# Where a mean aggregation's two projections are computed, and who casts its adjacency, in a four-block graph network

## What is computed

```python
x = x + gnn0(layernorm(x), adj)        # attention over the graph
x = x + ffn0(layernorm(x))             # 64 experts' routing with capacity 256, one shared feed-forward
x = x + gnn1(layernorm(x), adj)
x = x + ffn1(layernorm(x))             # 8 experts, top 2

def ffn0(h):    # idx, p: two best of softmax(h @ router_w.T); keep: place in its expert < 256
    y = gelu(h @ w1.T + b1) @ w2.T + b2                      # 256 -> 1024 -> 256
    return y * sum_over_two(where(keep, p, 0))

def gnn1(h, adj):
    deg = adj.sum(axis=1, keepdims=True) + 1e-5
    return relu((adj / deg) @ h @ W_neigh.T + b_neigh + h @ W_self.T + b_self)

def ffn1(h):    # w = softmax over the two best logits of h @ Wg + bg
    a, g = split(h @ W1[e] + b1[e]); return sum_e w_e * ((silu(a) * g) @ W2[e] + b2[e])
```

## Time and profile before

| | us |
|---|---|
| three runs | 1263.65, 1255.98, 1261.61 |
| median | 1261.61 |
| profiled execution, its own time | 1258.48 |
| its span | 1256.6 |
| attention | to 405 |
| feed-forward, ahead of its chunk loop | 405 to 431 |
| feed-forward, chunks and the end behind them | 431 to 596.4 |
| self projection | 596.4 to 640.9 |
| aggregation, to its last product | 640.9 to 840.4 |
| aggregation, behind its last product | 840.4 to 886.8 |
| experts and combination | 886.8 to 1256.6 |

### The profile page before, as it was taken

The page is one execution under the profiler, slowest core; times in us unless marked ns, Lnnn a source line. Parts: engine busy times, 40 slices in busy tenths (PEclk is TensorE's granted clock), DMA queues, the critical chain, the costliest instruction groups (busy, mean ns, idle before and its releaser), DMA issues. The chain is left out here.

```text
span 1256.6 us, 24125 instructions
## 1 busy us (share of the span) xinstructions
PE 1058.0 (84%) x7768; PEld 857.3 (68%) x7769; DVE 848.2 (67%) x1916; ACT 691.8 (55%) x752; POOL 121.2 (10%) x122
## 2 busy tenths in 40 slices
PE   4759999999999799898789999981199999999930
PEld 3548888888888688787568888871056666666620
DVE  7469999999994656766734676675255565565526
ACT  2669999999982777774455555530033333333310
POOL 1000000000000000000000132224011211211210
PEclk9889999999999699999889999995599999999975
DMA  9937777777700212110357678721621111111127
GB/s 286 286 113 229 218 246 216 234 224 220 242 18 1 77 68 101 68 35 1 126 210 290 263 285 309 296 89 64 261 111 54 50 54 54 50 54 54 47 85 261
DMA packets 71546, 186.91 MB, mean 149 GB/s; under 512 B 7777, under 2 KB 57824, under 8 KB 62144
## 3 DMA queue, kind: packets, MB, share of 16 engines
q1 hardware_dynamic: 51152, 138.38, 33.5%
q10 hardware_dynamic: 11616, 29.76, 6.5%
q0 software_dynamic: 8720, 17.99, 4.9%
HBM read 140.75 MB, written 45.35 MB: 148 GB/s over the span
## 5 line engine op out<-in xcount | busy, mean ns | idle before, releaser
L586 PE MATMUL PS<-G,PT 128*128 128x256 f16 x2028 | 230.3, 273 | 0.0
L586 PEld LDWEIGHTS PS<-G,PT 128*128 128x128 f16 x2028 | 198.8, 98 | 22.8
L1343 PE MATMUL sum<-H,adjTh 128*128 128x257 f16 x676 | 154.4, 276 | 7.7 <-ACT adjTh L1290 7.7
L1345 PE MATMUL sum<-H,adjTh 128*128 128x256 f16 x676 | 154.4, 275 | 0.0
L1748 DVE SCALAR_TENSOR_TENSOR hb<-ePsH,w_unscale,eb 128x1024 f32<-128x1024 f32 x59 | 75.7, 1284 | 86.4 <-PE ePsH L1669 86.4
L1669 PE MATMUL ePsH<-W,xT_hi 128*128 x472 | 122.5, 382 | 4.7 <-DVE xT_lo L1739 4.7
L1705 ACT ACTIVATE xT_hi<-ePsX 128x256 f16<-128x256 f32 x59 | 22.6, 384 | 177.6 <-PE ePsX L1658 177.6
L1689 PE MATMUL ePsY<-W,actT 128*128 x472 | 111.6, 380 | 0.2 <-issue 0.2
L573 PE MATMUL PS<-ident,probs 128*128 128x128 f32 x676 | 90.0, 280 | 22.2 <-DVE PT L434 20.5
L434 DVE SCALAR_TENSOR_TENSOR PT<-PS,PT 128x1024 f16<-128x1024 f32 x104 | 103.4, 1016 | 4.4 <-ACT PT L283 4.4
L573 PEld LDWEIGHTS PS<-ident,probs 128*128 128x128 f32 x676 | 76.3, 144 | 31.9 <-issue 23.9
(11 more groups left out here) (271 smaller groups left out, 1931.2 us busy)
## 6 DMA issues: line engine op xcount, KB each, us to landing
adjf<-adj_dram SPq DMA_DIRECT2D x26, 1664.0 KB, 8.2
adjTf<-adjT_dram SPq DMA_DIRECT2D x26, 1664.0 KB, 8.7
slot_rows<-blank SPq DMA_DIRECT2D x26, 1028.0 KB, 11.2
c_w<-eW_dram ACTq DMA_DIRECT2D x8, 1024.0 KB, 5.0
xs<-slot_rows SPq DMA_DIRECT2D x59, 128.5 KB, 2.0
d_stage<-eW_dram ACTq DMA_DIRECT2D x7, 1024.0 KB, 8.0
results<-results_dram ACTq DMA_DIRECT2D x12, 512.0 KB, 9.4
eb<-eb_dram SPq DMA_DIRECT2D x1, 4096.0 KB, 13.9
```

What stands on the lines that cost most here:

```text
L586: mm = nc.tensor.matmul(acc[u][:, 0:D], left, right, start=(j == 0 and n == 0), stop=(j == T - 1 and n == 2))
L1343: nc.tensor.matmul(acc[u][:, 0:D + 1], left, H[:, j, 0:D + 1], start=(j == 0), stop=False, skip_group_check=True)
L1345: mm = nc.tensor.matmul(acc[u][:, 0:D], left, H[:, j, D + 2:2 * D + 2], start=False, stop=(j == T - 1), skip_group_check=True)
```

## The change

What it does, in five parts:

1. The program `normalised_projection` is gone. `capacity_ffn` loads W_self and W_neigh (side by side in `wsn`, 512 columns) and their biases, takes their norm in the same sum as the others, and splits them. For each pair of tiles r = 0 to 12: `residual(r)` with the moments, `row_deviation` (a square root on ScalarE), `normalise_rows`, `turn_rows` (four transpositions into psT), `rows_hi` (ScalarE) and `rows_lo` (VectorE), `project_rows` (for each tile six products 512 columns wide into psR[s], s = 0 or 1, one buffer for each tile of the pair), `neighbour_hi` (ScalarE) and `own_and_lo` (VectorE), which write the projected neighbour rows into H and the self projection with biases into `own`. `row_group(c)` is the two pairs 2(c-8), 2(c-8)+1: in chunk c their residual and normalisation, in chunk c+1 the rest.
2. Aggregation multiplies the adjacency with the projected rows: `residual(i)` is sum times 1/degree plus `own`, then relu and addition to X. `turn_mean` and `project` go.
3. The adjacency is loaded by GpSimd's transfers from the f32 array straight into f16 buffers, four of them (`NADJ`), and the cast on ScalarE goes. GpSimd issues them from aggregation's own start, two loads ahead of each pair's scatters.
4. Behind the products the pairs follow at less distance; rows are normalised once into one of four buffers (`NROW`), the second copy is ScalarE's (`second_copy`); the counts have a PSUM tile of their own.
5. The experts' scales (`expert_ffn` changes in the index of `w_unscale` alone): one for all eight experts, from the columns' largest magnitudes (`expert_peak` on VectorE, chunks 2 to 9) in place of the eight squares; the second weights' squares are new (`second_square`, ScalarE, chunks 10 and 11 and behind the loop). The first activation buffer G of the feed-forward is single in place of double, and its weights and row halves lie in the room of W1, which is allocated earlier; `own` and H serve as scratch.

The feed-forward's loops after it, cut:

```diff
+            def project_rows(r):
+                pe.wait_ge(rowT_lo, r + 1)
+                for s in range(2):
+                    wait(pe, own_ready, 2 * (r - 1) + s + 1)
+                    for n, (left, right) in enumerate(((0, 0), (0, 1), (1, 0))):
+                        for k in range(KD):
+                            mm = nc.tensor.matmul(psR[s][:, :], rowT[r % 2][left][:, k, s * P:(s + 1) * P],
+                                                  wsn_p[right][:, k, :], start=(n == 0 and k == 0),
+                                                  stop=(n == 2 and k == KD - 1))
+                    mm.then_inc(proj_done, 1)
...
-            for c in range(NCH + 1):
+            for c in range(NCH + 3):
                 for b in range(4):
                     if c < NCH:
                         if b == 0:
                             pe.wait_ge(lo_ready, c + 1)
                         hidden_part(c, b)
...
+                    for r in row_group(c - 1)[b % 2:b % 2 + 1]:
+                        if b < 2:
+                            turn_rows(r)
+                        else:
...
+                            project_rows(r)
...
-                    if c > 0:
+                    if 0 < c <= NCH:
...
                         output_part(c - 1, b)
```

ScalarE in chunk c:

```diff
                 gelu(c, 0)
                 gelu(c, 1)
                 gelu_hi(c, 0)
...
-                if 2 <= c < 2 + E1:
-                    expert_square(c - 2)
...
+                if c == 10:
+                    second_square(0)
+                if c == 11:
+                    second_square(1)
...
+                for r in row_group(c - 1)[0:1]:
+                    rows_hi(r)
+                for r in row_group(c - 2)[1:2]:
+                    neighbour_hi(r)
                 gelu(c, 2)
                 gelu_hi(c, 1)
                 gelu(c, 3)
                 gelu_hi(c, 2)
+                for r in row_group(c - 1)[1:2]:
+                    rows_hi(r)
                 gelu_hi(c, 3)
+                for r in row_group(c - 1)[0:1]:
+                    neighbour_hi(r)
+                row_deviation(c)
```

VectorE in chunk c:

```diff
                 gelu_lo(c, 1)
...
-                if c >= 8:
-                    residual(4 * c - 32, 4 * c - 30)
+                if 2 <= c < 2 + E1:
+                    expert_peak(c - 2)
+                for r in row_group(c - 2)[1:2]:
+                    own_and_lo(r)
+                for r in row_group(c - 1)[0:1]:
+                    rows_lo(r)
+                for r in row_group(c)[0:1]:
+                    residual(r)
                 gelu_lo(c, 2)
...
-                if c >= 8:
-                    residual(4 * c - 30, 4 * c - 28)
+                for r in row_group(c - 1)[1:2]:
+                    rows_lo(r)
+                for r in row_group(c)[1:2]:
+                    residual(r)
                 gelu_lo(c, 3)
+                for r in row_group(c - 1)[0:1]:
+                    own_and_lo(r)
...
+                invert_deviation(c)
+                for r in row_group(c):
+                    normalise_rows(r)
```

Aggregation:

```diff
-                dve.wait_ge(proj_ready, t + 1)
-                v.tensor_tensor(own[:, t, :], psF[u][:, 0:D], own[:, t, :], ALU.add).then_inc(out_ready, 1)
+                dve.wait_ge(rdeg_ready, i + 1)
+                v.scalar_tensor_tensor(own[:, i, :], acc[u][:, 0:D], rdegree[u][:, :], own[:, i, :], ALU.mult,
+                                       ALU.add).then_inc(out_ready, 1)
...
+            def load(i):
+                if live(i):
+                    wait(pool, acc_ready, i - NADJ + 1)
+                    pool.dma_start(adjh[i % NADJ][:, :], adjv[i, :, :]).then_inc(adj_in[i % NADJ], 16)
...
+            for i in range(NADJ - 1):
+                load(i)
+            for i in range(0, TOTAL, 2):
+                load(i + NADJ - 1)
+                load(i + NADJ)
+                if live(i - 6):
+                    scatter(i - 6)
```

More of the change, by code:

```diff
@@ new lines, in normalise_rows, with rows_lo @@
+            def normalise_rows(r):
+                dve.wait_ge(row_ready, r // 2 + 1)
+                wait(dve, rows_turned, r - 1)
+                for s in range(2):
+                    i = 2 * r + s
+                    v.tensor_scalar(h[:, r % 2, s, :], X[:, i, :], moments[:, i, 0:1], row_rstd[:, i:i + 1], ALU.subtract,
+                                    ALU.mult).then_inc(rows_done, 1)
+            def rows_lo(r):
+                dve.wait_ge(rowT_hi, r + 1)
+                v.scalar_tensor_tensor(rowT[r % 2][1][:, :, :], psT[r % 2][:, :].rearrange("p (k n) -> p k n", k=KD), H_SCALE,
+                                       rowT[r % 2][0][:, :, :], ALU.mult, ALU.subtract).then_inc(rowT_lo, 1)
@@ L1264, in mean_aggregation @@
+        slots_ready, token_ready, copy_ready = sem("d_slots"), sem("d_token"), sem("d_copy")
+        scattered = [sem(f"d_scattered{q}") for q in range(NROW)]
+        stage_in, split_hi, split_done = sem("d_stage_in"), sem("d_split_hi"), sem("d_split")
         block = ctx.enter_context(nc.Block())
@@ L1332, in _, with deviation, second_copy @@
-            act.wait_ge(ones_set, 1)
-            for i in range(0, TOTAL, 2):
-                body(i)
+            def deviation(i):
+                act.wait_ge(moments_ready, i + 2)
+                wait(act, rstd_ready, i // 2)
+                nc.scalar.activation(std[:, :], moments[(i // 2) % 2][:, :, 1], ACT.Sqrt, bias=eps[:, :]).then_inc(std_ready, 1)
+            def second_copy(i):
+                act.wait_ge(h_ready, i + 2)
+                for u in range(2):
+                    nc.scalar.copy(rows[:, row_slot(i), u, 1, 0:D], rows[:, row_slot(i), u, 0, 0:D]).then_inc(copy_ready, 1)
@@ L1336, in _, with products @@
         @block.tensor
         def _(pe):
-            def products(t, u):
-                pe.wait_ge(half_ready, t + 1)
-                wait(pe, agg_ready, t - 1)
-                for j in range(T):
-                    left = adjh[u][:, j * P:(j + 1) * P]
+            def products(i, first, last):
+                u = i % 2
+                if first == 0:
+                    pe.wait_ge(adj_in[i % NADJ], 16 * (i // NADJ) + 16)
+                    wait(pe, out_ready, i - 1)
+                for j in range(first, last):
+                    left = adjh[i % NADJ][:, j * P:(j + 1) * P]
@@ L1453, in row_norm @@
[L1453 to L1459 removed]
+                    dve.wait_ge(stats_done, i + u + 1)
@@ L1503, in write_slots @@
[L1503 to L1507 removed]
+                m = i // 2
```

757 lines of the change are left out of this document (391 added, 366 removed).

## The result

The changed kernel took 1316.53 us, the median of four runs (1315.12 to 1318.29), the kernel before 1259.94 (1255.98 to 1263.65): a ratio of 1.045, 95% interval 1.041 to 1.049. It is 4.5% slower; 1293 us, 2.5% slower, was forecast, with a range of 1228 to 1345.

The account below looks back on a forecast made before the run. Bounds were read by stage: VectorE routing in chunks 5 and 6, TensorE in chunks 8 to 11 and, nearly throughout, aggregation. Terms 3 + 5.5 + 68.5 + 12 + 31.5 - 85.5 gave +35 on 1258.5: 1293 us, range 1228 to 1345.

Parts of the forecast that it names:

- front and maxima: Ahead of chunk 8: +3 us for loading, squaring and splitting the projection weights, +5.5 for the expert maxima on VectorE.
- chunks 9 to 12, clock included: Projections in these feed-forward chunks: 110.5 us instead of 42, +68.5, and 12 more for the half clock.
- behind the loop: After the feed-forward's last hidden part: five more pairs to project, 45 us instead of 13.6, +31.5 (20 to 40).
- projection program: Self projection of 44.5 us removed; a barrier and the first adjacency tile's wait leave 10 us: -34.5.
- aggregation: Aggregation without turn_mean, project and the ScalarE casts: 13.0 us a pair of tiles, -35 in all.
- behind the last product: Routing and scatters after aggregation's last product: 30 us instead of 46.4, -16.
- The two waits: TensorE stands ahead of project_rows in chunks: 6.7 us for own_and_lo (second pair), 4.8 for rows_lo (first pair).
- The clock: Half clock on TensorE after idle times in chunks 9 to 12: 12 us (0 to 16) for seven waits.
- The square root's table: ScalarE table switches in chunks 8 to 12: root ready at 8.4 us, needed at 11.8, so only chunk 9 pays.
- The cast at the accumulating rate: Rival: casting adjacency transfers run at the accumulating load's 190 GB/s, aggregation takes 107 us more, 1400 us; chance 0.10.
- The cast 10 to 20% short: Rival: casting adjacency transfers some 10 to 20% below the plain rate, 1308 to 1348 us; chance 0.14.
- The rival on the other side: Rival: projections find operands ready, a chunk costs TensorE's 16.6 us, the tail 30: 1222 us, 3.1% faster; chance 0.16.

Follow-up runs that it names:

- pipeline: Changed kernel with project_rows, transpositions, residuals and square root reordered in the queues, in the chunks and behind the loop: 1251.5 us, ratio 0.993 to the kernel before.
- first_wait: Changed kernel with TensorE's project_rows of each group's second pair one chunk later, behind output_part(c-1,1): 1311.3 us.
- maxima_moved: Changed kernel with the expert maxima of chunks 4, 5 and 6 taken in chunks 7 to 9, both in-loop squares in chunk 11: 1310.1 us.
- late_wait: Changed kernel with TensorE and VectorE waiting for aggregation's small tables one pair of tiles later: 1310.9 us.
- tables_early: Changed kernel with aggregation's five small tables loaded by SyncE at the end of its list in the feed-forward's program: 1309.5 us.
- double_loads: Changed kernel loading each adjacency tile a second time into a buffer nobody reads: 1405.4 us.
- best: Changed kernel with pipeline and tables_early, maxima spread over chunks 2 to 11, second weights' squares in chunk 12 and behind the loop: 1239.3 us.
- second_wait: Changed kernel with VectorE's rows_lo of the first pair and own_and_lo of the pair before ahead of gelu_lo(c,1): 1292.6 us.
- plain_loads: Changed kernel with adjacency loaded as f32 by SyncE and cast on ScalarE, two f16 buffers in place of four: 1383.7 us.

## Why the prediction was right, and where its sizes were off

The direction and the mechanism held, the size did not quite: +35 us on the profiled 1258.5 (2.8%; the 2.5% set 1293 against a median 3 us higher) was forecast, +56.7 measured. The measured time is inside the range, but that is partly luck in how the range was drawn. The changed kernel's own range was "1270 to 1315 where its transfers keep up", they did keep up, and 1316.5 is just above it; the room up to 1345 was meant for a slow cast, which did not come. The sign "chunks of 25 to 30 us" was missed too: from one wait of 6.23 us to the next it is 33.8, 34.1 and 31.7 us. Term by term, forecast and measured change:

| term | forecast | measured |
|---|---|---|
| front and maxima | +8.5 | +10.9 |
| chunks 9 to 12, clock included | +80.5 | +88.4 |
| behind the loop | +31.5 | +29.5 |
| projection program | -34.5 | -33.9 |
| aggregation | -35 | -23.8 |
| behind the last product | -16 | -13.9 |
| experts | 0 | -0.5 |
| sum | +35 | +56.7 |

- **The two waits.** "TensorE stands 6.7 us" and "4.8 us": 6.23 and 5.95 (5.95 with the square in its chain, for which 6.4 was forecast; 4.55 in chunk 12 without it). In chunks 9 to 12 TensorE is idle 46.6 us and busy 41.8 longer, some 24.4 of it added work (4 times 6.1, as forecast); the rest, some 17, is the clock. That the order causes the waits is shown by pipeline, which changes the order alone, in the chunks and behind them, and is 65 us faster; the forecast had put waits, clock and their part of the tail at 71.
- **The clock.** "I take 12 us (0 to 16) for seven" was too small. A chunk's same products took 21.66 us busy in the changed kernel and 16.76 in pipeline, 4.9 us for two waits, so 2.45 a wait on average where 1.7 was taken, some 17 in all. The row I used was of a stand of 2 us; these are of 6 us and have wide products behind them, and which of the two makes the difference was not tried. This is most of the 7.9 us by which chunks 9 to 12 were under-priced; the rest is chunk 9, where turn_rows waited 6.09 us for its first rows and I had 3.5.
- **The square root's table.** The result was "needed at 11.8 us": true as long as the first wait stood. first_wait shows what lies behind it: turn_rows, whose rows need that root, then waits 5.09 us.
- **Maxima.** +5.5 forecast, 7.8 by maxima_moved: all three in chunks 4 to 6 were paid in full (2.28 us each) with 1 us more, where I had taken half for chunk 4. The 7.8 rests on one profiled execution of each kernel; against the slower ones named below it would be some 10. On table loads: in the kernel after, a load at 621.37 took 1.28 us, the square root began at 622.66 and took 0.30, and the load back began at 622.98, so again no drain is in these rows, against the 2.66 us that the Trainium skill, page "ScalarE: Activation LUTs", section "What ACT_TABLE_LOAD costs", gives for a switch.
- **Aggregation, the term that was furthest off.** "I take 13.0 a pair and -35 in all." The rate was right (12.96), the total was not: 13 pairs at 13.0 are 169, and that is 30.5 less than 199.5, not 35. Nor do the parts named reach 35: 28 for turn_mean and project and most of 5.9 for the casts. The 4.5 between them have the size of the wait for the first cast, which lies ahead of this stage and is in the 44.5 us of the projection program already:

```profile
640.86 0.37 PE L1343 MATMUL sum<-H,adjTh 128*128 128x257 f16 x1 [4.50 <-ACT adjTh L1290]
```

The other 6.5, from 169 to 175.5: 4.5 for the small tables, which late_wait and tables_early remove (5.6 and 7 us), and 2.3 for the first tile, whose 52 products took 8.06 us, the first 20 of them at half clock, as in the kernel before. Here lie half of the 22 us by which the sum fell short.
- **Projection program, tail, scatters.** -33.9, +29.5 and -13.9 for -34.5, +31.5 and -16.
- **The rivals.** The cast at the accumulating rate had 0.10 and is excluded by double_loads. The cast 10 to 20% short had 0.14 and the range 1308 to 1348, in which the measured 1316.5 lies; it is not what happened. From 761.3 to 911.3 TensorE is busy all of 150.0 us, so it waits for no tile, and double_loads gives the rate. The rival on the other side (1222, the waits are not there) is wrong for the order as written. With the order mended the change takes 1251.5 (pipeline), and 1239.3 in best, which also moves maxima, squares and the small tables.

One reading of the table above needs care. The stretch up to the end of hidden_part(8,3) took 139.1 us in the changed kernel and 141.4 to 142.0 in second_wait, first_wait, late_wait, plain_loads and double_loads, whose instructions are the same up to there. The granted clock accounts for it. The same 20 us of the changed kernel, then of second_wait:

```profile
520.00:540.00 20.00, 16.85 (x160) 14.16 (x159) 11.80 (x13) 8.10 (x15) 0.00 (x0) 0.96 0.16 53
```

```profile
520.00:540.00 20.00, 16.86 (x137) 13.37 (x136) 11.04 (x12) 6.51 (x12) 0.00 (x0) 0.81 0.06 14
```

TensorE is busy as long in both but gets 160 products done at 0.96 and 137 at 0.81; the 23 missing ones are about 2.5 us at 0.109 each. In both kernels it had stood 3.15 us at 533 to 534 us, and the next product took 0.39 us in one and 0.61 in the other. So the +10.9 of the front would be some 13 in the other executions, and a single stage's difference of 2 to 3 us between two profiled executions can be clock alone.

What is still open: whether ScalarE could cast in another place, and why one and the same stand is followed by the full clock in one execution and by the half clock in another.

## What to carry to other kernels

Work that is moved into idle slots of a full pipeline is priced by its place in each in-order queue, not by its engine time: here 6 us of TensorE's work a chunk cost 23, and nearly the same instructions in another order 7. Here project_rows stood directly behind hidden_part(c,3), from which its own operand came by way of ScalarE and VectorE, and TensorE stood for the whole chain. Write that chain down for each new wait, and put the consumer as many parts later as the chain is long. And take a wait away only together with the next one behind it: first_wait won 5 us (9 up to the start of aggregation), second_wait 24, both together 35.5, and with the third 65.

## What the hardware showed that was not expected

- Small transfers issued beside large casting ones landed late. Four of the tables of 8 to 32 KB, issued half a microsecond apart, landed 5.1, 12.1, 15.8 and 18.8 us after their issue; taken with their issue times (726.71, 727.69, 728.16, 729.50) that is at 731.8, 739.8, 744.0 and 748.3, up to some 4 us from one table to the next in the list (one more stands between the first two and one between the last two). That is about the time of one casting tile, 4.7 us or less in double_loads. In other kernels with the same loads TensorE's wait for them was 4.1 to 9.25 us. With plain adjacency loads issued behind them in the same list they took 3.8 to 4.9 us. Whether the cast or the order does it is not shown. The Trainium skill, page "DMA: Bandwidth & Descriptors", section "Queues, rings and completion order", says that an engine takes turns between queues, a packet at a time; by that alone, as I read it, a small table would not wait for a whole tile; the rows show up to a tile's time or so for each table, so by this reading that rule alone does not give these times.
- The casting transfer reads about as fast as a plain one moves (365 GB/s or more by the estimate above, against 382), though the rows of the profile count only the bytes written.
- A stand of 6 us cost 2.45 us, the mean of two in a chunk, by the half clock that followed it, where one of 2 us had cost 1.6. After one of 3.15 us the products ran at the full clock in the changed kernel and at the half clock in second_wait.
